# The split tables of the TensorE picks in another layout: the part index outermost

## The chip, the core and the metric

The kernel runs on one core of a Trainium2 chip. Its engines are TensorE (PE, with its weight load shown apart as PEld), VectorE (DVE), ScalarE (ACT), GpSimd (POOL) and SyncE (SP); each has its own queue of instructions, and they meet through semaphores. The metric is the device time of one execution in microseconds, as the median of several runs.

## The reference, cut to what matters

A graph of 12500 nodes (64 features) and 400000 edges, sorted by destination. Two layers follow each other, each with a residual and a layer norm:

```python
h    = x @ W_lin + b_lin
agg1 = mean over edges into a node of h[src]
h    = tanh(agg1 @ W1_agg + h @ W1_root + b1)            # 16 wide
agg2 = mean over edges into a node of h[src]
x    = layernorm(x + tanh(agg2 @ W2_agg + h @ W2_root + b2))
hn   = x @ Wn.T + bn
w    = ssp(ssp(edge_attr @ We1.T + be1) @ We2.T + be2)   # per edge, 64 wide
agg  = segment_sum(hn[src] * w, dst)
x    = layernorm(x + (ssp(agg @ Wc.T + bc) @ Wp.T + bp))
```

So rows of a node table are fetched by `src` three times (tables p1, h1 and hn) and added up by `dst`.

## The kernel before

The edges are cut into 125 blocks (`NB`) of 128 partitions x 25 slots. Three phases go over all blocks: `pick_phase("e1")` on the p1 table, `pick_phase("e2")` on the h1 table (both 16 numbers a row), `gate_phase("e3")` on the hn table (64 numbers). Phase A before e1 builds the p1 table, phase B between e1 and e2 the h1 table, phase C between e2 and e3 the first layer norm and the hn table, phase D the output.

The row of an edge's source is fetched in one of two ways. For the first 15 slots of a block in the pick phases (23 in the gate phase) GpSimd issues one indirect DMA a slot from DRAM (L612, L886). For the last 10 slots (`SEL`; `GSEL` = 2 in the gate phase) TensorE picks the row from a copy of the table in SBUF, by one-hot matmuls. The 98 rows that a partition holds (`NQ`) stand in `split_sb` (`hn_split` in the gate phase), padded to 100 in the pick phases. Each number is split into two parts (upper 12 bits of the fraction, and the rest), so that a matmul of type fp32r is exact. A row index q is taken as two digits: in the pick phases h = q mod 4 and a = q div 4 (25 values). For each h and each part one matmul streams the 25 rows of that h (400 columns) against the one-hot weight `low_hot[:, h]` and adds into one PSUM bank (L667, 8 matmuls a slot); a ninth (L670) streams `others`, 400 numbers in one run, against `hi_hot` and pushes the 24 rows that are not a down by a large number; VectorE then takes the maximum over a (`take`, L719). In the gate phase h = q mod 7, a = q div 7 (14 values, in two halves of 7 rows, 448 columns, into two banks, L921, 28 matmuls a slot), and VectorE masks and sums over a. In `split_sb` of before, the two parts of a row lie side by side and rows are in order, so what a matmul reads is 25 runs of 16 numbers, 128 numbers apart; in `hn_split` 7 runs of 64.

The digits are made once by VectorE in phase A (L446 to L476), turned by TensorE and stored as f16 rows (`sel_dram`, `gate_dram`). Per block SyncE loads them broadcast over partitions, ScalarE makes `low_hot` (four `Abs` activations on L633, one `Relu` on L637), VectorE makes `hi_hot` (L712).

The fetched and picked rows are added up by destination: VectorE writes one-hot tiles `hot` of 13 and 12 slots for a window of 128 destinations (L739, `make_hot`), TensorE multiplies the rows with them (`add_up`, L685, 25 matmuls of 128 columns), VectorE adds the sum into `acc` (L765). A block whose destinations span two windows has two visits, with 50 matmuls; how many a block has is read at run time. The later a block, the wider its destinations are spread.

The order of TensorE's work is written out by hand. In the body of block n: `pick(0, n+1)`, then `add_up(n)`, then `pick(1)`, `pick(2)`, `pick(3)` of n+1, the four groups having 3, 2, 3 and 2 slots (`SIZE`). VectorE's body: first one-hot tile of n, `take(3, n)`, `high_hots`, the split of the picked rows into bf16 parts (L725 to L731), the visits, then `take(0)` to `take(2)` of n+1. GpSimd's gathers go up to four blocks ahead in the pick phases (two in the gate phase) and wait for `block_used`; `add_up(n)` waits for the gathers of block n.

`table_rows` (L246) writes both the bf16 rows for DRAM and `split_sb`; the gate phase's `hn_split` is written on L1376 (VectorE) and L1412 (ScalarE).

Of the kernel before, what the change touches and what calls it, by code (L numbers as in the profile page):

```python
# [24 lines left out]
F = 64  # L25
# [59 lines left out]
def gnn_kernel(nc, x, xw, src, src_sel, dst_all, edge_t, W_linT, b_lin, W1_agg, W1_root, b1, W2_parts, W2_diag, WnT, bn, We1T, be1,  # L85
               We2T, be2, WcT, bc, WpT, bp, out):
    ctx = ExitStack()
    with ctx:
# [108 lines left out]
        split_sb = mid.enter_context(nc.sbuf_tensor("split_sb", [P, HI1 * HI2, 2 * H], F32R))  # L197
# [48 lines left out]
        def table_rows(dve, v, rows, split, top_i, low_n, made):  # L246
# [9 lines left out]
            dve.tensor_copy(split[..., 0:H], top_i.bitcast(F32))  # L256
            dve.drain()
            dve.tensor_copy(part(MID), low_n)
            dve.tensor_tensor(split[..., H:2 * H], v, top_i.bitcast(F32), ALU.subtract)
# [29 lines left out]
        with nc.Block() as block:  # L289
# [135 lines left out]
            def _(dve):  # L425
# [7 lines left out]
                for w in range(2):  # L433
# [8 lines left out]
                dve.tensor_scalar(split_sb[:, NQ:, :].rearrange("p a c -> p (a c)"), others_f[:, 0:4, :]  # L442
                                  .rearrange("p a f -> p (a f)"), 0.0, None, ALU.mult)
# [15 lines left out]
                dve.tensor_single_scalar(gate_i[:, :, :], sel_a_i[:, SEL - GSEL:, :], 147, ALU.mult)  # L459
                dve.drain()  # L460
                dve.tensor_single_scalar(gate_i[:, :, :], gate_i[:, :, :], 10, ALU.arith_shift_right)
                dve.drain()
                dve.tensor_copy(gate_hi[:, :, :].rearrange("p n j -> p j n"), gate_i[:, :, :])
                dve.drain()
                dve.scalar_tensor_tensor(gate_low[:, :, :], gate_hi[:, :, :].rearrange("p n j -> p j n"), -float(GLOW),
                                         sel_q[:, SEL - GSEL:, :], ALU.mult, ALU.add)
                dve.drain()
                dve.scalar_tensor_tensor(gate_low[:, :, :], gate_low[:, :, :], float(P), sel_digit[0][:, SEL - GSEL:, :],
                                         ALU.mult, ALU.add)
                dve.tensor_single_scalar(sel_a_i[:, :, :], sel_a_i[:, :, :], HI2.bit_length() - 1, ALU.arith_shift_right)  # L470
# [3 lines left out]
                dve.scalar_tensor_tensor(sel_q[:, :, :], sel_digit[1], -float(HI2), sel_q[:, :, :], ALU.mult, ALU.add)  # L474
                dve.drain()
                dve.scalar_tensor_tensor(sel_digit[0], sel_q[:, :, :], float(P), sel_digit[0], ALU.mult, ALU.add)  # L476
# [4 lines left out]
                for c in range(2):  # L481
                    if c == 1:
# [8 lines left out]
                               halves(split_sb[:, 0:NQ, :])[:, :, a:b, :],  # L491
# [51 lines left out]
        def pick_phase(tag, table, buf, hots, tiles):  # L543
# [33 lines left out]
            with nc.Block() as block:  # L577
# [75 lines left out]
                def _(pe):  # L653
# [4 lines left out]
                    def pick(gr, n):  # L658
# [3 lines left out]
                        for k in range(SIZE[gr]):  # L662
                            e = slice(k * P, (k + 1) * P)
                            o = bank[BANK0[gr] + k][:, 0:PICK]
                            for h in range(HI2):
                                for part in range(2):
                                    pe.matmul(o, low_hot[gr][:, h, e],  # L667
                                              split_sb[:, h:HI1 * HI2:HI2, part * H:(part + 1) * H],
                                              start=(h == 0 and part == 0), stop=False)
# [120 lines left out]
        def gate_phase(tag, table, buf, hots, tiles):  # L790
# [52 lines left out]
            with nc.Block() as block:  # L843
# [49 lines left out]
                def _(pe):  # L893
# [21 lines left out]
                    def pick(n, s):  # L915
                        pe.wait_ge(low_made, GSEL * n + s + 1)
                        pe.wait_ge(pick_taken, GSEL * n + s + 1)
                        for h in range(GLOW):
                            for part in range(2):
                                for c in range(2):  # L920
                                    last = pe.matmul(bank[c][:, 0:GHALF * F], low_hot[s][:, h, :],  # L921
                                                     hn_split[:, c * GHALF * GLOW + h:(c + 1) * GHALF * GLOW:GLOW,
# [727 lines left out]
```

## Time and profile before

| | us |
|---|---|
| median of 3 runs | 9292.74 |
| lowest and highest | 9292.62, 9294.54 |
| span of the profiled execution | 9281.8 |
| median less span | 10.9 |

| engine | busy us | share of the span | instructions |
|---|---|---|---|
| PE | 8512.6 | 92% | 52035 |
| PEld | 7831.7 | 84% | 52036 |
| DVE | 6294.8 | 68% | 7500 |
| ACT | 5654.9 | 61% | 10182 |
| POOL | 6536.9 | 70% | 6717 |

The span runs from the first to the last instruction of one profiled execution; its own time as a run is not given apart. The busy time of PE is modelled at its ends: matmuls are pipelined, so the mean of one (358 ns for L667) is longer than the distance between the starts of two; where a distance is meant, it is read from starts. The phases lie at about 71 to 2665 us (e1), 2737 to 5330 us (e2) and 5470 to 9210 us (e3). The granted TensorE clock is a share of 2.4 GHz; its mean over the span is 0.952.

### The profile page before, as it was taken

Reading aid. Unit: us, or ns where it says so; the run is one execution under the profiler, and the core shown is the slowest. Engines: PE = TensorE matmul, PEld = TensorE weight load, DVE = VectorE, ACT = ScalarE, POOL = GpSimd, SP = SyncE. Lnnn points to the kernel's source line nnn. Section 1 sums busy time; section 2 is a strip of 40 time slices with the busy share of each in tenths; the row PEclk is TensorE's granted clock in tenths of the full one; section 3 lists DMA queues with packets and bytes.
Section 4 is the critical chain, followed back from the end, with each engine's and each line's share of the span. In section 5 each row is a group of like instructions: output and inputs, shape, how many; then the busy total and the mean of one; then the engine's idle time right before and its main releaser. Section 6 shows DMA issues by size and latency. Waiting matters only on the chain. (4 is left out here: it accounts for less than half of the span.)

```text
span 9281.8 us, 165856 instructions
## 1 busy us (share of the span) xinstructions
PE 8512.6 (92%) x52035; PEld 7831.7 (84%) x52036; DVE 6294.8 (68%) x7500; ACT 5654.9 (61%) x10182; POOL 6536.9 (70%) x6717
## 2 busy tenths in 40 slices
PE   8999999988889999999898878888888888999998
PEld 7999999888889999998888867677777777888887
DVE  6666666767756666667767766666666666777777
ACT  5666666555546666665555456666666666666665
POOL 5777777756637777777666447777777777777776
PEclk9999999999989999999999979999999999999998
DMA  2222222111112222222111122222222222222222
GB/s 74 50 48 48 49 49 48 40 38 39 39 30 51 48 48 50 48 48 45 41 36 39 28 76 54 57 57 57 53 57 57 57 57 54 57 57 57 53 57 57
DMA packets 385189, 466.16 MB, mean 50 GB/s; under 512 B 174821, under 2 KB 253241, under 8 KB 384742
## 3 DMA queue, kind: packets, MB, share of 16 engines
q0 software_dynamic: 212000, 156.07, 10.9%
q1 hardware_dynamic: 172804, 309.29, 10.2%
q8 instruction: 32, 0.52, 0.0%
q14 instruction: 31, 0.25, 0.0%
q10 hardware_dynamic: 322, 0.03, 0.0%
HBM read 451.33 MB, written 13.55 MB: 50 GB/s over the span
## 5 line engine op out<-in xcount | busy, mean ns | idle before, releaser
L667 PE MATMUL banks<-split_sb,e_low_hot 128*128 128x400 f32 x20000 | 4283.7, 358 | 28.8 <-ACT e_low_hot L637 28.8
L667 PEld LDWEIGHTS banks<-split_sb,e_low_hot 128*128 128x128 f32 x20000 | 3799.5, 192 | 70.5 <-ACT e_low_hot L637 29.2
L886 POOL DMA_INDIRECT big<-hn_table,src_i x2875 | 2852.3, 992 | 884.8 <-issue 869.3
L637 ACT ACTIVATE e_low_hot<-e_key_off 128x1536 fp32r<-128x1536 f16 x1000 | 1272.2, 1272 | 1854.6 <-PE banks L670 1823.5
L612 POOL DMA_INDIRECT big<-p_table,src_i x1875 | 1806.7, 964 | 785.1 <-issue 559.0
L612 POOL DMA_INDIRECT big<-h_table,src_i x1875 | 1806.3, 963 | 727.3 <-issue 554.7
L719 DVE TENSOR_REDUCE picked<-banks 128x48 f32<-128x1200 f32 x1000 | 1194.2, 1194 | 1205.1 <-PE banks L670 1202.3
L633 ACT ACTIVATE e_key_off<-e_key_in,node_off 128x384 f16<-128x384 f16 (+1 forms) x4000 | 1920.9, 551 | 103.5 <-DMA e_hi_in<-sel_dram 21.9
L739 DVE SCALAR_TENSOR_TENSOR hot<-dst_f,win_base,banks 128x1536 bf16<-128x1536 f32 (+1 forms) x934 | 1762.3, 1896 | 308.8 <-issue 180.1
L921 PE MATMUL banks<-hn_split,e_low_hot 128*128 128x448 f32 x7000 | 1488.1, 369 | 73.5 <-issue 68.0
L921 PEld LDWEIGHTS banks<-hn_split,e_low_hot 128*128 128x128 f32 x7000 | 1299.5, 188 | 202.0 <-issue 63.8
L938 PEld LDWEIGHTS banks<-hot,big 128*64 128x64 f32 x8550 | 929.7, 137 | 155.0 <-issue 122.8
L938 PE MATMUL banks<-hot,big 128*64 128x128 f32 x8550 | 982.8, 274 | 49.6 <-DVE acc L1117 30.0
L1080 DVE SCALAR_TENSOR_TENSOR hot<-dst_f,win_base,banks 128x1664 f32<-128x1664 f32 (+1 forms) x467 | 885.2, 1896 | 178.0 <-PE banks L938 126.2
L670 PE MATMUL banks<-others,e_hi_hot 128*128 128x400 f32 x2500 | 866.2, 346 | 0.0
L685 PE MATMUL banks<-hot,big 128*64 128x128 bf16 x8550 | 600.7, 226 | 245.4 <-DVE acc L765 153.3
L904 PE MATMUL banks<-e_wide,we 128*128 128x512 f32 x1000 | 546.5, 709 | 298.4 <-DVE e_wide L1046 288.4
L685 PEld LDWEIGHTS banks<-hot,big 128*64 128x64 bf16 x8550 | 516.3, 114 | 355.7 <-DVE hot L739 271.5
L970 ACT ACTIVATE e_wide<-e_wide 128x512 f32<-128x512 f32 x500 | 268.9, 538 | 859.3 <-DVE e_wide L1046 859.3
L999 ACT ACTIVATE e_low_hot<-e_key_in,node_off 128x128 fp32r<-128x128 f16 x1750 | 537.0, 387 | 348.4 <-PE banks L921 346.9
L904 PEld LDWEIGHTS banks<-e_wide,we 128*128 128x128 f32 x1000 | 253.7, 262 | 538.0 <-DVE e_wide L1046 353.4
L1092 DVE SCALAR_TENSOR_TENSOR big<-e_wide,big 128x1600 f32<-128x1600 f32 x125 | 228.3, 1826 | 643.2 <-DMA big<-hn_table,src_i 639.2
(212 smaller groups left out, 5936.4 us busy)
## 6 DMA issues: line engine op xcount, KB each, us to landing
e_wide<-in_edge_t SPq DMA_DIRECT2D x125, 832.0 KB
e_key_in<-sel_dram SPq DMA_DIRECT2D x250, 320.0 KB
e_hi_in<-sel_dram SPq DMA_DIRECT2D x250, 320.0 KB
big<-hn_table,src_i POOLq DMA_INDIRECT x2875
big<-p_table,src_i POOLq DMA_INDIRECT x1875
big<-h_table,src_i POOLq DMA_INDIRECT x1875
e_key_in<-gate_dram SPq DMA_DIRECT2D x125, 64.0 KB
src_i<-in_src SPq DMA_DIRECT2D x375, 12.5 KB, 1.7
```

What stands on the lines that cost most here:

```text
L612: pool.indirect_dma_start(buf[u][:, j, 0:ROW0], None, table, bass.IndirectOffsetOnAxis(ap=src_i[u][:, j:j + 1], axis=0),).then_inc(gathere ...
L633: act.activation(off[:, h, :], key_in[u][:, es], ACT.Abs, bias=node_off[:, h:h + 1])
L637: act.activation(low_hot[gr][:, :, :], off, ACT.Relu, bias=1.0, scale=-1.0).then_inc(low_made, 1)
L667: pe.matmul(o, low_hot[gr][:, h, e], split_sb[:, h:HI1 * HI2:HI2, part * H:(part + 1) * H], start=(h == 0 and part == 0), stop=False)
L670: last = pe.matmul(o, hi_hot[gr][:, e], others[:, :, :], start=False, stop=True)
L685: last = pe.matmul(sums[0:ROW0, 0:WIN], buf[u][:, j, :], hots[h][:, j - a, :], start=(j == 0), stop=(j == SLOTS - 1))
L719: dve.tensor_reduce(picked[:, AT[gr]:AT[gr] + SIZE[gr], :], found, AX.X, ALU.max).then_inc(pick_taken, 1)
L739: dve.scalar_tensor_tensor(hots[h], d.unsqueeze(2).to_broadcast([P, b - a, WIN]), win_base[:, bass.ds(window, 1)], iota_ps.unsqueeze(1).to ...
L886: pool.indirect_dma_start(buf[u][:, j, 0:F], None, table, bass.IndirectOffsetOnAxis(ap=src_i[u][:, j:j + 1], axis=0),).then_inc(gathered[u ...
L921: last = pe.matmul(bank[c][:, 0:GHALF * F], low_hot[s][:, h, :], hn_split[:, c * GHALF * GLOW + h:(c + 1) * GHALF * GLOW:GLOW, part * F:(p ...
L938: last = pe.matmul(sums[0:F, 0:WIN], buf[u][:, j, 0:F], hots[h][:, j - a, :], start=(j == 0), stop=(j == SLOTS - 1))
L1080: dve.scalar_tensor_tensor(hots[h], d.unsqueeze(2).to_broadcast([P, b - a, WIN]), win_base[:, bass.ds(window, 1)], iota_ps.unsqueeze(1).to ...
```

## The change

Both split tables get the part index outermost and the rows of one h next to each other: `split_sb[:, part, row, :]` and `hn_split[:, part, row, :]`. For the rows of one h to be neighbours while the table itself stays in order, the digits change places: h = q div 25 and a = q mod 25 in the pick phases, h = q div 14 and a = q mod 14 in the gate phase. So the digits are computed by other constants (41/1024 is 1/25, 2341/32768 is 1/14 for these q). A matmul then reads rows h * 25 to h * 25 + 24 of one part. The number of matmuls, their columns and their order stay the same. The diff is whole.

```diff
@@ -194,7 +194,7 @@
         root = mid.enter_context(nc.sbuf_tensor("root", [P, NQ, H], F32))
         h1_deg = mid.enter_context(nc.sbuf_tensor("h1_deg", [P, NQ, H + 1], F32))
         deg = mid.enter_context(nc.sbuf_tensor("deg", [P, NQ], F32))
-        split_sb = mid.enter_context(nc.sbuf_tensor("split_sb", [P, HI1 * HI2, 2 * H], F32R))
+        split_sb = mid.enter_context(nc.sbuf_tensor("split_sb", [P, 2, HI1 * HI2, H], F32R))
 
         banks = pb("banks", [P, 8 * 512])
         bank = [banks[:, i * 512:(i + 1) * 512] for i in range(8)]
@@ -253,10 +253,10 @@
             dve.tensor_single_scalar(top_i, v.bitcast(I32), TOP12, ALU.bitwise_and)
             dve.drain()
             dve.tensor_tensor(low_n, v, part(HI), ALU.subtract)
-            dve.tensor_copy(split[..., 0:H], top_i.bitcast(F32))
+            dve.tensor_copy(split[0], top_i.bitcast(F32))
             dve.drain()
             dve.tensor_copy(part(MID), low_n)
-            dve.tensor_tensor(split[..., H:2 * H], v, top_i.bitcast(F32), ALU.subtract)
+            dve.tensor_tensor(split[1], v, top_i.bitcast(F32), ALU.subtract)
             dve.drain()
             dve.tensor_tensor(part(LO), low_n, part(MID), ALU.subtract).then_inc(made, 1)
 
@@ -439,8 +439,8 @@
                 dve.tensor_copy(bias_wide[:, :, :], bias_1[:, :].unsqueeze(1).to_broadcast([1, 16, 2 * H])).then_inc(a_w, 1)
                 dve.wait_ge(consts, 1)
                 dve.tensor_copy(others[:, :, :], others_f)
-                dve.tensor_scalar(split_sb[:, NQ:, :].rearrange("p a c -> p (a c)"), others_f[:, 0:4, :]
-                                  .rearrange("p a f -> p (a f)"), 0.0, None, ALU.mult)
+                dve.tensor_scalar(split_sb[:, :, NQ:, :], others_f[:, 0:2 * (HI1 * HI2 - NQ), :]
+                                  .rearrange("p (s a) f -> p s a f", s=2), 0.0, None, ALU.mult)
                 dve.wait_ge(sel_src_in, 16)
                 src_n = sel_src_i.rearrange("p (j n) -> p j n", n=NB)
                 dve.tensor_single_scalar(sel_p_i, sel_src_i, 1, ALU.arith_shift_right)
@@ -456,24 +456,26 @@
                 dve.drain()
                 dve.tensor_copy(sel_a_i[:, :, :], sel_q[:, :, :])
                 dve.drain()
-                dve.tensor_single_scalar(gate_i[:, :, :], sel_a_i[:, SEL - GSEL:, :], 147, ALU.mult)
-                dve.drain()
-                dve.tensor_single_scalar(gate_i[:, :, :], gate_i[:, :, :], 10, ALU.arith_shift_right)
-                dve.drain()
-                dve.tensor_copy(gate_hi[:, :, :].rearrange("p n j -> p j n"), gate_i[:, :, :])
-                dve.drain()
-                dve.scalar_tensor_tensor(gate_low[:, :, :], gate_hi[:, :, :].rearrange("p n j -> p j n"), -float(GLOW),
+                dve.tensor_single_scalar(gate_i[:, :, :], sel_a_i[:, SEL - GSEL:, :], 2341, ALU.mult)
+                dve.drain()
+                dve.tensor_single_scalar(gate_i[:, :, :], gate_i[:, :, :], 15, ALU.arith_shift_right)
+                dve.drain()
+                dve.tensor_copy(gate_low[:, :, :], gate_i[:, :, :])
+                dve.drain()
+                dve.scalar_tensor_tensor(gate_hi[:, :, :].rearrange("p n j -> p j n"), gate_low[:, :, :], -float(GHIGH),
                                          sel_q[:, SEL - GSEL:, :], ALU.mult, ALU.add)
-                dve.drain()
                 dve.scalar_tensor_tensor(gate_low[:, :, :], gate_low[:, :, :], float(P), sel_digit[0][:, SEL - GSEL:, :],
                                          ALU.mult, ALU.add)
-                dve.tensor_single_scalar(sel_a_i[:, :, :], sel_a_i[:, :, :], HI2.bit_length() - 1, ALU.arith_shift_right)
+                dve.tensor_single_scalar(sel_a_i[:, :, :], sel_a_i[:, :, :], 41, ALU.mult)
+                dve.drain()
+                dve.tensor_single_scalar(sel_a_i[:, :, :], sel_a_i[:, :, :], 10, ALU.arith_shift_right)
                 dve.drain()
                 dve.tensor_copy(sel_digit[1], sel_a_i[:, :, :])
                 dve.drain()
-                dve.scalar_tensor_tensor(sel_q[:, :, :], sel_digit[1], -float(HI2), sel_q[:, :, :], ALU.mult, ALU.add)
-                dve.drain()
-                dve.scalar_tensor_tensor(sel_digit[0], sel_q[:, :, :], float(P), sel_digit[0], ALU.mult, ALU.add)
+                dve.scalar_tensor_tensor(sel_q[:, :, :], sel_digit[1], -float(HI1), sel_q[:, :, :], ALU.mult, ALU.add)
+                dve.scalar_tensor_tensor(sel_digit[0], sel_digit[1], float(P), sel_digit[0], ALU.mult, ALU.add)
+                dve.drain()
+                dve.tensor_copy(sel_digit[1], sel_q[:, :, :])
                 dve.drain()
                 dve.sem_inc(sel_digits, 1)
 
@@ -488,7 +490,7 @@
                     a, b = ACUT[c], ACUT[c + 1]
                     dve.wait_ge(a_p1, c + 1)
                     table_rows(dve, halves(p1_n[:, :, :])[:, :, a:b, :], halves(tab[:, :, :])[:, :, a:b, :],
-                               halves(split_sb[:, 0:NQ, :])[:, :, a:b, :],
+                               [halves(split_sb[:, part, 0:NQ, :])[:, :, a:b, :] for part in range(2)],
                                top[:, 0:2 * (b - a), :].rearrange("p (w i) h -> p w i h", w=2),
                                low[:, 0:2 * (b - a), :].rearrange("p (w i) h -> p w i h", w=2), a_tab)
 
@@ -664,8 +666,7 @@
                             o = bank[BANK0[gr] + k][:, 0:PICK]
                             for h in range(HI2):
                                 for part in range(2):
-                                    pe.matmul(o, low_hot[gr][:, h, e],
-                                              split_sb[:, h:HI1 * HI2:HI2, part * H:(part + 1) * H],
+                                    pe.matmul(o, low_hot[gr][:, h, e], split_sb[:, part, h * HI1:(h + 1) * HI1, :],
                                               start=(h == 0 and part == 0), stop=False)
                             last = pe.matmul(o, hi_hot[gr][:, e], others[:, :, :], start=False, stop=True)
                         last.then_inc(pick_psum, 1)
@@ -919,8 +920,7 @@
                             for part in range(2):
                                 for c in range(2):
                                     last = pe.matmul(bank[c][:, 0:GHALF * F], low_hot[s][:, h, :],
-                                                     hn_split[:, c * GHALF * GLOW + h:(c + 1) * GHALF * GLOW:GLOW,
-                                                              part * F:(part + 1) * F],
+                                                     hn_split[:, part, h * GHIGH + c * GHALF:h * GHIGH + (c + 1) * GHALF, :],
                                                      start=(h == 0 and part == 0), stop=(h == GLOW - 1 and part == 1))
                         last.then_inc(pick_psum, 1)
 
@@ -1198,7 +1198,7 @@
                     if c > 0:
                         dve.wait_ge(b_h, c)
                         a, b = BCUT[c - 1], BCUT[c]
-                        table_rows(dve, root[:, a:b, :], tab[:, a:b, :], split_sb[:, a:b, :], top[:, 0:b - a, :],
+                        table_rows(dve, root[:, a:b, :], tab[:, a:b, :], [split_sb[:, part, a:b, :] for part in range(2)], top[:, 0:b - a, :],
                                    low[:, 0:b - a, :], b_tab)
 
             @block.scalar
@@ -1254,7 +1254,7 @@
         f_out = sem("f_out")
         f_store = [sem(f"f_store{b}") for b in range(2)]
         hn_held = ExitStack()
-        hn_split = hn_held.enter_context(nc.sbuf_tensor("hn_split", [P, NQ, 2 * F], F32R))
+        hn_split = hn_held.enter_context(nc.sbuf_tensor("hn_split", [P, 2, NQ, F], F32R))
         f_top = sem("f_top")
         f_hi = sem("f_hi")
         f_xb = sem("f_xb")
@@ -1373,7 +1373,7 @@
                     dve.tensor_single_scalar(t, hn_o[g % 2][:, 0:b - a, :].bitcast(I32), TOP12,
                                              ALU.bitwise_and).then_inc(f_top, 1)
                     dve.drain()
-                    dve.tensor_tensor(hn_split[:, a:b, F:2 * F], hn_o[g % 2][:, 0:b - a, :], t.bitcast(F32), ALU.subtract)
+                    dve.tensor_tensor(hn_split[:, 1, a:b, :], hn_o[g % 2][:, 0:b - a, :], t.bitcast(F32), ALU.subtract)
 
                 for g in range(NGQ + 2):
                     if g < NGQ:
@@ -1409,7 +1409,7 @@
                     if g >= 3:
                         a, b = group(g - 3)
                         act.wait_ge(f_top, g - 2)
-                        act.copy(hn_split[:, a:b, 0:F], top_i[(g - 3) % 2][:, 0:b - a, :].bitcast(F32)).then_inc(f_hi, 1)
+                        act.copy(hn_split[:, 0, a:b, :], top_i[(g - 3) % 2][:, 0:b - a, :].bitcast(F32)).then_inc(f_hi, 1)
 
             @block.gpsimd
             def _(pool):
```

## Rows read from the trace of the kernel before

**Rows 1.** The page, part 1: busy us (share of the span) xinstructions.

```profile
PE 8512.6 (92%) x52035; PEld 7831.7 (84%) x52036; DVE 6294.8 (68%) x7500; ACT 5654.9 (61%) x10182; POOL 6536.9 (70%) x6717
```

**Rows 2.** The page, part 5: costliest groups, count, busy us, mean ns, idle before.

```profile
L667 PE MATMUL banks<-split_sb,e_low_hot 128*128 128x400 f32 x20000 | 4283.7, 358 | 28.8 <-ACT e_low_hot L637 28.8
...
L886 POOL DMA_INDIRECT big<-hn_table,src_i x2875 | 2852.3, 992 | 884.8 <-issue 869.3
...
L612 POOL DMA_INDIRECT big<-p_table,src_i x1875 | 1806.7, 964 | 785.1 <-issue 559.0
...
L921 PE MATMUL banks<-hn_split,e_low_hot 128*128 128x448 f32 x7000 | 1488.1, 369 | 73.5 <-issue 68.0
...
L685 PE MATMUL banks<-hot,big 128*64 128x128 bf16 x8550 | 600.7, 226 | 245.4 <-DVE acc L765 153.3
```

**Rows 3.** Timeline, phase e1, one-visit blocks: start us, duration us, engine, line.

```profile
102.29 0.91 PE L685 MATMUL banks<-hot,big 128*64 128x128 bf16 x13
...
88.85 0.96 POOL L612 DMA_INDIRECT big<-p_table,src_i  x1 [0.30 <-issue]
...
1461.24 1.63 PE L685 MATMUL banks<-hot,big 128*64 128x128 bf16 x25
...
1458.41 0.98 POOL L612 DMA_INDIRECT big<-p_table,src_i  x1 [0.30 <-issue]
```

**Rows 4.** Timeline of PE, phase e1, first matmul of five add-ups of two visits.

```profile
2072.59 0.30 PE L685 MATMUL banks<-hot,big 128*64 128x128 bf16 x2
...
2095.53 0.24 PE L685 MATMUL banks<-hot,big 128*64 128x128 bf16 x1
...
2261.97 0.24 PE L685 MATMUL banks<-hot,big 128*64 128x128 bf16 x1
...
2287.65 0.24 PE L685 MATMUL banks<-hot,big 128*64 128x128 bf16 x1
...
2574.43 0.35 PE L685 MATMUL banks<-hot,big 128*64 128x128 bf16 x3
```

**Rows 5.** Timeline of DVE in the same stretch.

```profile
2238.60 1.95 DVE L739 SCALAR_TENSOR_TENSOR hot<-dst_f,win_base,banks 128x1664 bf16<-128x1664 f32 x1 [0.54 <-PE banks L685]
```

**Rows 6.** Timeline of PE: one add-up of two visits, and the pick after it.

```profile
2237.53 1.58 PE L685 MATMUL banks<-hot,big 128*64 128x128 bf16 x25
...
2243.93 1.04 PE L667 MATMUL banks<-split_sb,e_low_hot 128*128 128x400 f32 x2
```

**Rows 7.** Windows: length, busy us (xcount) by engine, PEclk, DMA share, GB/s.

```profile
2218.65:2222.06 3.41, 3.41 (x15) 3.22 (x13) 3.08 (x4) 0.00 (x0) 1.43 (x2) 0.50 0.01 3
...
2266.45:2273.25 6.80, 6.30 (x27) 6.10 (x28) 4.25 (x5) 0.00 (x0) 2.86 (x3) 0.50 0.04 5
...
2338.15:2341.50 3.35, 2.94 (x17) 2.76 (x18) 3.25 (x4) 0.00 (x0) 0.22 (x1) 0.50 0.00 0
```

**Rows 8.** Windows by stage: phase e1 in two parts, and phase e3.

```profile
75.00:1580.00 1505.00, 1491.22 (x9126) 1452.30 (x9126) 1032.64 (x1270) 1027.03 (x1609) 1143.16 (x1188) 1.00 0.21 49
...
1580.00:2665.00 1085.00, 976.55 (x6350) 939.05 (x6350) 760.05 (x859) 569.29 (x891) 660.50 (x685) 0.95 0.16 37
...
5470.00:9210.00 3740.00, 3322.06 (x19710) 2844.50 (x19711) 2494.75 (x2884) 2346.47 (x5001) 2852.30 (x2875) 0.94 0.24 56
```

**Rows 9.** Timeline of PE: one pick of nine matmuls in phase e1.

```profile
2256.79 1.69 PE L667 MATMUL banks<-split_sb,e_low_hot 128*128 128x400 f32 x8
2258.31 0.35 PE L670 MATMUL banks<-others,e_hi_hot 128*128 128x400 f32 x1
2258.49 1.68 PE L667 MATMUL banks<-split_sb,e_low_hot 128*128 128x400 f32 x8
```

**Rows 10.** Timeline of PE: one pick of phase e3.

```profile
6005.49 5.92 PE L921 MATMUL banks<-hn_split,e_low_hot 128*128 128x448 f32 x28
```

**Rows 11.** Timeline of DVE in phase A.

```profile
21.07 0.81 DVE L472 CAST hot<-sel_a_i 128x1250 f32<-128x1250 int32 x1
...
29.16 0.56 DVE L252 CAST a_tab<-p_n 128x768 bf16<-128x768 f32 x1 [4.20 <-ACT p_n L368]
```

## The prediction

> **What bounds the kernel now.** I read the page's groups first, then the windows by stage, then single blocks in the timeline of TensorE, GpSimd and VectorE. By share of the span TensorE is the bound: busy 92% [rows 1], and half the span is the 20000 pick matmuls of L667, with 7000 more on L921 [rows 2]. The share is an average over stages with different limits, so I ask in each stage what ends last.
>
> Stage one, pick phases, blocks of one visit (two thirds of each phase). GpSimd issues 15 gathers a block. In a pick phase they are 1806.7 us busy and 559.0 us idle in "issue", the fixed pause between two of them [rows 2], so 2365.7 / 1875 = 1.262 us each and 18.9 us a block; counted over whole blocks the beat is 19.02. TensorE needs a little less: at the start its add-up begins 102.29 - 88.85 = 13.4 us behind the last gather's issue of its block, 72 blocks later 1461.24 - 1458.41 = 2.8 us behind [rows 3]. So its block is (1461.24 - 102.29) / 72 = 18.87 us, it catches up 0.15 us a block, and at 2.8 us it meets the gather's landing and from there keeps GpSimd's pace. It is already at that floor before the two-visit blocks begin.
>
> Stage two, the blocks of two visits. 8550 matmuls on L685 are 342 visits of 25 [rows 2]; 250 blocks in two phases, so 92 blocks have two. Here a block takes (2574.43 - 2072.59) / 21 = 23.90 us [rows 4], more than GpSimd's 19, so GpSimd runs four buffers ahead and waits. A block without a drop of the clock takes 2095.53 - 2072.59 = 22.94 us [rows 4]. In it TensorE is the bound: all ten picks stand in its chain, and VectorE's hot tile for the second visit waits 0.54 us for TensorE's first add-up [rows 5]. During the add-ups TensorE works little: two bursts of 25 short matmuls from 2237.53 to about 2243.9, waiting for VectorE between them [rows 6]. There the granted clock falls to its low level of 1.2 GHz for 3.4 or 6.8 us [rows 7], and what falls on picks runs at half pace: the block that starts at 2237.53 lasts 24.44 us, to 2261.97 [rows 4], so one drop costs 1.5 us. The stage's clock is 0.95, stage one's 1.00 [rows 8].
>
> Stage three, the gate phase: 2875 gathers, 2852.3 us busy plus 869.3 in "issue" of 884.8 idle [rows 2] = 3721.6 us of a stage of 3740 [rows 8]. GpSimd never waits for anybody here worth naming. TensorE's picks on L921 are hidden.
>
> **What the change removes.** The spacing of the picks, start to start. Eight strided matmuls of L667 go from 2256.79 to 2258.31, 0.190 each; the one of L670, which reads 400 numbers in one run from `others`, is followed after 2258.49 - 2258.31 = 0.18 us [rows 9]. On L921, 28 matmuls of 448 columns in 7 runs: (5.92 - 0.37) / 27 = 0.206, the first of them longer, so about 0.204 for the others [rows 10]; scaled by columns to 400 that is 0.182. So one run or seven cost about the same per column, and 25 runs some 7 ns more. I take 0.183 us for the changed L667, by the nearest row, L670: 6.5 ns x 8 = 52 ns a pick, 0.52 us a block. Bounds: 0 from above (the spacing has another cause, below). From below the pace of L685, 128 columns in (1.58 - 0.22) / 24 = 0.057 us [rows 6], times 400/128 = 0.177: 13 ns each, 1.04 us a block. A loss I cannot exclude from a row, but every operand in one run that the trace has is the faster one.
> L921: from 7 runs to one I take 0; the bound is the same 0.177 per 400 columns, 5 ns a matmul, and hidden behind GpSimd at any size.
>
> **Where that lies.** In stage one it lies beside GpSimd's gathers. TensorE catches up 0.15 + 0.52 = 0.67 us a block instead of 0.15, meets the landing after some 16 blocks instead of 72, and then waits. The two-visit blocks start at the same time as now: 0. What is late next is the gather. If that cover were gone, 158 blocks x 0.52 = 82 us would count.
> In stage three: 0, same cover.
> In stage two it is on the chain, all ten picks: VectorE's slack of 0.54 us [rows 5] must take the 0.26 us of the five picks between VectorE's take and the first add-up, and does. That is 92 x 0.52 = 48 us at an unchanged clock, and here is the step that I weigh most. The low stretches begin at 2218.65, 2266.45 and 2338.15 [rows 7]: 47.80 = 2 x 23.90 and 71.70 = 3 x 23.90 us apart, and 23.90 is also the mean block. Blocks of 22.94, 24.44 and (with a drop of 6.8 us) 2287.65 - 2261.97 = 25.68 us [rows 4] alternate so that their mean stays on this beat: a block without a drop comes early to the next one, whose add-up then lies where it earns a drop, and is set back. That is a regulator: what picks save brings more drops. With the change a block without a drop is 22.94 - 0.52 = 22.42, one with a single drop 22.42 + 1.5 = 23.92: still the beat, now with a drop in nearly every block instead of in some 60%. So I forecast that the clock takes the 48 us back but for about 3. It holds only by a hair: 1 ns of spacing is 80 ns a block, and 23.92 stands against 23.90.
>
> **The small edits.** The key digits: VectorE does one 1250-wide shift and one 1250-wide copy more (the multiply takes the place of a shift, and a copy is added), 2 x 0.81 = 1.6 us [rows 11], before L252, where VectorE waits 4.20 us for ScalarE [rows 11]: 0, cover left 2.6 us; uncovered it would be 1.6 us once. The splits are written with as many elements by as many instructions (L256, L259, L1376, L1412), and 768 wide they take what any such copy takes, so 0, and in any case between -1 and +1 us for all of them. The zeroing of the spare rows is one instruction as before. The host's side and all DMAs are unchanged. GpSimd's pace is a touch quicker where TensorE waits for it; some 50 more blocks in that state, at 0.03 to 0.06 us each, are 2 to 3 us.
>
> Sum: 3 + 3 = 6 us. The span of the profiled execution is 9281.8 us; the median of the runs lies 10.9 us above it, for what lies around the span, so 9275.8 + 10.9 = 9286.7 us. Its own range: 9276 to 9293.
>
> **A rule against the change.** L670 against L667 shows a difference of some 7 ns [rows 9]. The Trainium skill, "SBUF — State Buffer", Specifications (TRN2), says that SBUF is read in lines of 16 bytes and that full speed needs two or more hits in a line, each change of line costing something. A run of 16 numbers of 4 bytes is four full lines, so old and new layout touch the same 100 lines with four hits each. By that rule the spacing stays at 190 ns and the time at about 9292.
>
> **The rivals.**
> 1. No change of spacing, chance 0.17. L670 and L921 differ from L667 in more than their runs: the matmul after each of them writes another PSUM bank, while the eight of L667 accumulate into one. If that is the 6.5 ns, the layout does nothing. For it: position is confounded with run length in every row I have. Against: L685 accumulates into one bank at 0.057 per 128 columns [rows 6] and shows no such extra. Time 9292, 9289 to 9296. The line rule above would give this too.
> 2. The beat lets go, chance 0.31. If the new spacing is below about 182.5 ns, a block with one drop is shorter than 23.90, and the add-ups drift through the beat; many blocks get no drop at all. With none, a block is 22.42: (23.90 - 22.42) x 92 = 136 us; with drops in as many blocks as now, 48 us. Middle 80 us: 9213, from 9160 to 9265. For it: 22.42 + 1.5 is only just the beat, and L921 scaled gave 0.182. Against: L670's row at 0.18 to 0.19 within its rounding.
> 3. Slower, chance 0.08. The pick before the add-up ends earlier while VectorE's chain stays, so TensorE's thin stretch of 6.4 us grows by 0.26. If this makes the low stretch 6.8 us instead of 3.4 in a third of the two-visit blocks, each pays 25.68 - 24.44 = 1.24 us more: 31 x 1.24 = 38 us: 9324. From 15 blocks on it is slower by over 0.2%. For it: such double drops are there now [rows 7]. Against: a double drop sets the block far back, and the next one has none.
> 4. The forecast, chance 0.44.
>
> **How the numbers follow.** A measurement here can tell about 0.2%, 18.6 us, from no change. Faster: rival 2 nearly whole and the edge of the forecast, 0.33. Slower: rival 3 and a little for what I don't see, 0.09. Same: 0.58. Time 9286. Range 9190 to 9300: it leaves out the far half of rival 2 and rival 3. Forecast and rival 1 alone: 9276 to 9296.
>
> **What would show it.** Eight matmuls of L667 in 1.47 us instead of 1.52 (right), still 1.52 (rival 1), under 1.46 (rival 2's door). TensorE behind GpSimd's last issue by 2.8 us from about block 16. The two-visit block: mean 23.90 with granted clock under 0.95 (the regulator), mean near 22.5 to 23.3 and a higher clock (rival 2), above 24 (rival 3). The gate stage within a few us. I am wrong if the stage from 75 to 1580 us ends earlier by more than 5 us, for then GpSimd was not its floor.

## The result, and the profile after

The changed kernel takes 9205.86 us, median of 4 runs (9197.64 to 9214.44), against 9293.64 (9292.62 to 9294.78, 4 runs): ratio 0.9905 [0.9893, 0.9917], 88 us less. The forecast was 9286, so next to nothing gained, and that was wrong in kind. The time lies inside the range of 9190 to 9300 only because the range reached over rival 2, "the beat lets go" (9213, chance 0.31), and that is what happened. The profiled execution after took 9197.64 us.

The page of after, parts 1 and 5, against [rows 1, 2]:

```profile
PE 8324.8 (91%) x52035; PEld 7644.7 (83%) x52036; DVE 6283.8 (68%) x7502; ACT 5655.1 (62%) x10182; POOL 6542.3 (71%) x6717
...
L669 PE MATMUL banks<-split_sb,e_low_hot 128*128 128x400 f32 x20000 | 4091.5, 347 | 30.5 <-ACT e_low_hot L639 30.5
L887 POOL DMA_INDIRECT big<-hn_table,src_i x2875 | 2854.2, 993 | 884.1 <-issue 869.6
L922 PE MATMUL banks<-hn_split,e_low_hot 128*128 128x448 f32 x7000 | 1489.5, 369 | 73.3 <-issue 68.0
```

What moved is one row: L667, now L669, is busy for 192 us less. The kernel gains 88. The windows of after by stage (length, busy us by engine, PEclk, DMA share, GB/s) answer to [rows 8]:

```profile
75.00:1580.00 1505.00, 1436.74 (x9138) 1401.58 (x9138) 1027.09 (x1270) 1027.11 (x1609) 1142.69 (x1189) 1.00 0.21 49
1580.00:2617.00 1037.00, 933.40 (x6340) 894.52 (x6338) 759.68 (x858) 569.36 (x891) 661.71 (x684) 0.97 0.16 39
...
5383.00:9123.00 3740.00, 3325.13 (x19707) 2843.12 (x19708) 2494.07 (x2884) 2346.41 (x5001) 2854.18 (x2875) 0.94 0.23 56
```

Stage one: TensorE has 54 us less work in the same 1505 us, and it goes into waiting. Stage two: the same work is done in 1037 us instead of 1085, at a clock of 0.97 instead of 0.95. Stage three: 3740 us for the same gathers. Counted by starts, the first two-visit block of phase e1 begins 0.8 us earlier, and the last pick of the phase 47.6 us earlier. Here is that pick, in the timeline of TensorE before and after:

```profile
2663.66 0.34 PE L670 MATMUL banks<-others,e_hi_hot 128*128 128x400 f32 x1
```

```profile
2616.02 0.34 PE L671 MATMUL banks<-others,e_hi_hot 128*128 128x400 f32 x1
```

In phase e2 the one-visit blocks take 2.6 us more than before, and the last pick comes 87.0 us earlier. The gate phase takes 3729.6 us from its first to its last gather, before 3728.6. All of the gain is in the two-visit blocks.

A pick of after, timeline of TensorE, against [rows 9]; it starts again after 1.63 us, before after 1.70:

```profile
2101.90 1.61 PE L669 MATMUL banks<-split_sb,e_low_hot 128*128 128x400 f32 x8
2103.34 0.34 PE L671 MATMUL banks<-others,e_hi_hot 128*128 128x400 f32 x1
2103.53 1.61 PE L669 MATMUL banks<-split_sb,e_low_hot 128*128 128x400 f32 x8
```

Over all picks at full clock the spacing of two L669 is 180.6 ns (17027 of them), before 189.6. In the two-visit stage, the first matmuls of five add-ups in a row, against [rows 4]:

```profile
2116.63 0.91 PE L686 MATMUL banks<-hot,big 128*64 128x128 bf16 x13
...
2138.88 0.91 PE L686 MATMUL banks<-hot,big 128*64 128x128 bf16 x13
...
2161.12 0.91 PE L686 MATMUL banks<-hot,big 128*64 128x128 bf16 x13
...
2183.47 1.89 PE L686 MATMUL banks<-hot,big 128*64 128x128 bf16 x25
...
2207.26 1.75 PE L686 MATMUL banks<-hot,big 128*64 128x128 bf16 x25
```

Blocks of 22.25, 22.24, 22.35 and 23.79 us: three in a row with hardly a price for the clock, then one that pays 1.5 for a drop (a stretch in which the granted clock is at its low level). Before, the blocks swung around 23.90. Low stretches are still there, with the same level as in [rows 7] (windows of after):

```profile
2188.96:2192.37 3.41, 3.41 (x16) 3.21 (x14) 3.14 (x4) 0.00 (x0) 1.41 (x2) 0.51 0.02 2
2257.26:2260.67 3.41, 3.41 (x16) 3.22 (x14) 3.22 (x4) 0.00 (x0) 1.14 (x2) 0.51 0.00 0
2281.16:2284.57 3.41, 3.41 (x15) 3.22 (x13) 3.11 (x4) 0.00 (x0) 1.42 (x2) 0.51 0.01 2
```

The last two lie 23.90 us apart, as before; the first two 68.3, with free blocks between. Before there were 24 and 23 low stretches in the two pick phases, now there are 15 and 19.

### The profile page after: what moved, and what is told of

It is laid out like the page before. It is cut to its first block and busy times, and to the rows that moved or that the text cites. A ratio compares the mean times of both kernels' runs of the same rounds, so it can differ in the third digit from the quotient of the medians.

```text
span 9195.2 us, 165858 instructions
## 1 busy us (share of the span) xinstructions
PE 8324.8 (91%) x52035; PEld 7644.7 (83%) x52036; DVE 6283.8 (68%) x7502; ACT 5655.1 (62%) x10182; POOL 6542.3 (71%) x6717
## 5 line engine op out<-in xcount | busy, mean ns | idle before, releaser
L669 PE MATMUL banks<-split_sb,e_low_hot 128*128 128x400 f32 x20000 | 4091.5, 347 | 30.5 <-ACT e_low_hot L639 30.5
L669 PEld LDWEIGHTS banks<-split_sb,e_low_hot 128*128 128x128 f32 x20000 | 3668.5, 190 | 57.0 <-ACT e_low_hot L639 30.9
```

Source lines behind the costliest of these rows:

```text
L669: pe.matmul(o, low_hot[gr][:, h, e], split_sb[:, part, h * HI1:(h + 1) * HI1, :], start=(h == 0 and part == 0), stop=False)
```

## The experiments

Times are medians; the kernel before ran on the same chip each time. Theory A: the 25 runs cost the time by themselves. Theory B: something that came with them does (the order of the table, the distance of the runs, the new digits). Theory C, on top of either: the clock takes savings back up to some size.

**1. Only the outer order of the table, runs as before.** The kernel before, with part outermost:

```diff
-split_sb [P, HI1 * HI2, 2 * H]      read [:, h:HI1 * HI2:HI2, part * H:(part + 1) * H]
+split_sb [P, 2, HI1 * HI2, H]       read [:, part, h:HI1 * HI2:HI2, :]
```

> The kernel before with the part index outermost in the pick phases only and the old digits: a pick matmul reads 25 runs of 16 numbers, now 64 apart and not 128. Theory (the number of runs sets the spacing): still 0.189 to 0.190 us between picks, time 9285 to 9300. Rival (the part beside it, or the 128 apart, was the trouble): 0.181, time near 9206.

Measured: 9284.17 (9279.07 to 9285.58, 8 runs) against 9283.98: 0.9999 [0.9989, 1.0009]. Spacing 189.4 ns. The outer order does nothing, and neither does halving the distance between two runs from 128 numbers to 64. (The times of this experiment and the next lie a few us under what I expected, because I had set that from the first chip; on this one the kernel before takes 9284 and not 9293.)

**2. The new digits, but 25 runs, 32 numbers apart.** The changed kernel with the table as it was:

```diff
-split_sb[:, part, h * HI1:(h + 1) * HI1, :]
+split_sb[:, h * HI1:(h + 1) * HI1, part * H:(part + 1) * H]
```

> The changed kernel with the parts of split_sb side by side again, the new digits kept: 25 runs of 16 numbers, 32 apart. Theory (number of runs): 0.189 to 0.190 us between picks, 9285 to 9300. Rival (the exchange of the digits, so other one-hot weights, brought the gain): 0.181 and 9206. Rival (lines that the matmul skips cost, neighbouring ones do not): between 0.181 and 0.189.

Measured: 9281.97 (9279.35 to 9284.25, 8 runs): 0.9998 [0.9988, 1.0008]. Timeline of TensorE in this kernel and in experiment 1, one pick each:

```profile
2197.38 1.67 PE L669 MATMUL banks<-split_sb,e_low_hot 128*128 128x400 f32 x8
2198.88 0.34 PE L671 MATMUL banks<-others,e_hi_hot 128*128 128x400 f32 x1
2199.06 1.67 PE L669 MATMUL banks<-split_sb,e_low_hot 128*128 128x400 f32 x8
```

```profile
2151.54 1.68 PE L667 MATMUL banks<-split_sb,e_low_hot 128*128 128x400 f32 x8
2153.07 0.34 PE L670 MATMUL banks<-others,e_hi_hot 128*128 128x400 f32 x1
2153.24 1.68 PE L667 MATMUL banks<-split_sb,e_low_hot 128*128 128x400 f32 x8
```

1.68 and 1.70 us, against 1.63: one run alone is what matters (A). The mean spacing is 188.2 ns, so runs that lie nearer are 1.2 ns cheaper. That should be 0.13 us a block, 12 us in 92; the median moved 2, which the interval does not tell from nothing. Add-ups of two visits in this kernel, first matmuls:

```profile
2117.08 1.58 PE L686 MATMUL banks<-hot,big 128*64 128x128 bf16 x25
...
2141.38 1.58 PE L686 MATMUL banks<-hot,big 128*64 128x128 bf16 x25
...
2167.00 1.58 PE L686 MATMUL banks<-hot,big 128*64 128x128 bf16 x25
...
2189.82 0.91 PE L686 MATMUL banks<-hot,big 128*64 128x128 bf16 x13
...
2212.65 1.58 PE L686 MATMUL banks<-hot,big 128*64 128x128 bf16 x25
```

24.30, 25.62, 22.82, 22.83, and then the same four again: mean 23.89, as before 23.91. The regulator that I predicted is here, and it holds fully (C): the blocks show it, where the median alone could not.

**3. Half of the picks in one run.** In part 1 the rows of h and its partner alternate, part 0 is as changed:

```diff
-split_sb[:, part, h * HI1:(h + 1) * HI1, :]
+part 0: the same;  part 1: split_sb[:, 1, at:at + 2 * HI1, :].rearrange("p (a k) c -> p k a c", k=2)[:, h % 2]
```

> The changed kernel, but part 1 of split_sb is stored with two values of h interleaved row by row, so that four of the eight matmuls of a pick read 25 runs and four read one. Both theories give 0.185 us for the mean spacing. If the time follows the spacing (half of the change): 9293 - 44 = 9249. If the beat of 23.90 us holds the two-visit blocks until a block with one drop is shorter than the beat (22.94 - 0.36 + 1.45 = 24.03 is still longer): two-visit blocks of 23.85 to 23.90 with a drop in nearly each, time 9287 to 9294, no gain.

Measured: 9255.1 (9253.4 to 9259.7, 7 runs): 0.9968 [0.9957, 0.998]. The eight matmuls of a pick take 1.483 us, exactly the mean of experiment 2 (1.511) and of after (1.455): the cost is per strided matmul. Add-ups, first matmuls:

```profile
2111.39 1.70 PE L707 MATMUL banks<-hot,big 128*64 128x128 bf16 x25
...
2133.93 1.59 PE L707 MATMUL banks<-hot,big 128*64 128x128 bf16 x25
...
2158.01 1.59 PE L707 MATMUL banks<-hot,big 128*64 128x128 bf16 x25
...
2182.08 0.91 PE L707 MATMUL banks<-hot,big 128*64 128x128 bf16 x13
...
2206.09 1.90 PE L707 MATMUL banks<-hot,big 128*64 128x128 bf16 x25
...
2230.05 1.87 PE L707 MATMUL banks<-hot,big 128*64 128x128 bf16 x25
...
2253.97 0.91 PE L707 MATMUL banks<-hot,big 128*64 128x128 bf16 x13
```

22.54, then 24.08, 24.07, 24.01, 23.96, 23.92: each block pays a drop and glides onto 23.9 until one slips through, and three blocks of 22.55 follow. Of 86 two-visit blocks in the two phases 28 are free of a drop. The hold lets most of the saving through here, with a one-drop block of 24.0, where I had set full hold and no gain for anything over 23.90; the time is near the 9249 that I had set for the spacing alone. What the runs give for what the picks save: 12 us at constant clock gave 2, 37 (0.40 x 92) gave 29, and the whole change's 66 gave 74 (experiment 5) and 88.

**4. The gate table back to 7 runs of 64.** The changed kernel, with hn_split as before:

```diff
-hn_split[:, part, h * GHIGH + c * GHALF:h * GHIGH + (c + 1) * GHALF, :]
+hn_split[:, h * GHIGH + c * GHALF:h * GHIGH + (c + 1) * GHALF, part * F:(part + 1) * F]
```

> The changed kernel with only hn_split laid out as before (7 runs of 64 for the matmuls of the gate phase). Theory (GpSimd's gathers are the floor of the gate phase, and 7 runs cost no more than one): gate phase within 3 us of the changed kernel's, time 9198 to 9214. Rival (part of the gain is in the gate phase): more than 9220.

Measured: 9225.97 (9174.39 to 9227.67, 5 runs): 0.9938 [0.9922, 0.9955]. Its gate phase takes 29.80 us a block, after 29.85, and the spacing there is 203.65 ns, after 203.77: seven runs or one are the same. The median lies outside the 9198 to 9214 that I expected and above the 9220 that I had set for a gain in the gate phase. By the trace of its fastest run the 20 us to after's median are not the gate's. This kernel's pick phases are after's to the instruction, and its five runs spread over 53 us (9174, 9206, 9226, 9226, 9228). No trace of one of the slower runs was kept, so that their time too is lost in the pick phases is inferred. How often the add-ups slip past a drop differs from one execution to the next: the profiled one, the fastest at 9174, has 9 and 17 low stretches in its pick phases, against 15 and 19 in after's.

**5. The changed kernel again**, unchanged, on another chip, beside the next three.

> The changed kernel once more, on the chip of the three beside it. The drops are not held to a beat, so single executions should lie 10 to 40 us apart: median 9195 to 9225. Theory (the gate phase is no part of the gain): the same as the kernel with only the gate table laid out as before.

Measured: 9209.64 (9192.74 to 9220.23, 4 runs) against 9283.58: 0.9923 [0.9906, 0.9939]. Reproduced, spread 27 us; the kernel before spreads 8 in 13 runs there.

**6 and 7. Fill TensorE's thin stretches.** Four matmuls of 400 columns, whose result nobody reads, stand between the two bursts of each add-up, in the changed kernel and in the kernel before:

```diff
+if h == 1:
+    for _ in range(4):
+        pe.matmul(bank[5][:, 0:PICK], hi_hot[0][:, 0:P], others[:, :, :], start=True, stop=True)
```

> The changed kernel with four more matmuls of 400 columns between the two bursts of each add-up, into a PSUM bank that nobody reads, so that TensorE is not thinly loaded there; the result is the same. Theory (the drops of the clock in the two-visit blocks cost what lies above a block of 22.24 us): hardly a drop left in the pick phases, two-visit blocks of 22.2 to 22.4 instead of 22.9, one-visit blocks unchanged at 19.0 under GpSimd's gathers: 9130 to 9160. Rival (what lies above 22.24 us is not the clock): two-visit blocks longer by the fill, 9210 to 9280.

> The kernel before with the same four matmuls in each visit. Theory: two-visit blocks of 22.9 to 23.1 us with hardly a drop (23.88 without the fill), so that the spacing alone is worth 0.7 us a block between this and the changed kernel with the fill; but one-visit blocks go from 19.0 to about 19.6, as TensorE has only 0.15 us a block to spare there, so the time is 9200 to 9290.

Measured: 9197.64 (9196.28 to 9199.15, 4 runs), 0.991 [0.9893, 0.9926], and 9379.69 (9378.14 to 9381.24, 2 runs), 1.0105 [1.0085, 1.0125]. The windows of the two-visit stage, first of the filled changed kernel, then of the filled one before:

```profile
1600.00:2600.00 1000.00, 961.61 (x6529) 904.93 (x6527) 747.04 (x840) 566.53 (x887) 647.64 (x671) 1.00 0.17 40
```

```profile
1660.00:2700.00 1040.00, 1000.94 (x6596) 939.10 (x6596) 751.86 (x849) 565.72 (x886) 623.68 (x639) 1.00 0.16 38
```

The clock is 1.00 in both: it is the thin work around the add-ups that lets it fall. And with no drop, every block is alike. Add-ups, first matmuls, 15 blocks apart, in the same order:

```profile
1991.01 0.91 PE L690 MATMUL banks<-hot,big 128*64 128x128 bf16 x13
...
2330.49 0.69 PE L690 MATMUL banks<-hot,big 128*64 128x128 bf16 x9
```

```profile
2061.22 0.91 PE L689 MATMUL banks<-hot,big 128*64 128x128 bf16 x13
...
2411.45 0.74 PE L689 MATMUL banks<-hot,big 128*64 128x128 bf16 x10
```

339.48 / 15 = 22.63 and 350.23 / 15 = 23.35 us: the layout by itself is worth 0.72 us a block. Both forecasts of the time missed. For the filled changed kernel I had expected 9130 to 9160, from blocks of 22.2 to 22.4 us; the drops are gone, but the block is 22.63 and not the drop-free 22.24 of after, so the fill itself costs 0.4 us a block and takes back more than half of what the drops had cost. For the filled kernel before I had expected 9200 to 9290: the fill also stands in the one-visit blocks, where TensorE has next to no slack, and makes them 19.76 us, so that the two-visit stage starts 69 us later (add-up of block 78 at 1644.5 us, before at 1575.0). Twice 69, less 92 x (23.90 - 23.35) = 51, is 88 of the 96 us that it lost. With the new layout the same fill gives 19.04, just over GpSimd's pace. The filled changed kernel has the lowest median of all, 12 us under the changed one beside it, which the two intervals don't tell from nothing; it is steadier, with a spread of 3 us against 27.

**8. Two of 15 gathers left out (kernel before).** GpSimd's cover of stage one is taken away; the rows are set to zero.

```diff
-took = SLOTS - SEL
+took = SLOTS - SEL - 2
+dve.memset(buf[u][:, took:SLOTS - SEL, :], 0.0)
```

> The kernel before, leaving out two of the fifteen gathers of each block of the pick phases (their rows are left at zero). GpSimd then needs 16.5 us a block. Theory (one-visit blocks are under GpSimd, TensorE close below): one-visit blocks of 18.85 us in both pick phases, time some 2 x 3 us less, 9275 to 9290 and two-visit blocks at 23.9 as before.

Measured: 9269.3 (9263.26 to 9272.87, 8 runs): 0.9984 [0.9974, 0.9995], some 14 us less, more than I had set. In its timeline GpSimd now waits, for the sequencer of VectorE:

```profile
989.38 0.95 POOL L612 DMA_INDIRECT big<-p_table,src_i  x1 [2.60 <-DVEq L766]
990.64 0.95 POOL L612 DMA_INDIRECT big<-p_table,src_i  x1 [0.31 <-issue]
```

The one-visit block is 18.79 us, TensorE's own, where it was 18.87 beside the gathers; two-visit blocks stay at 23.91. So stage one before has two limits within 0.25 us: 18.79 for TensorE and 19.02 for GpSimd. A cheaper pick alone can move nothing there.

**9 to 12. Fill only in the gap between two visits, and 13 gathers with the new layout.** Seven fill matmuls after the first visit's add-up, none in one-visit blocks, in after, before and half; and experiment 8's edit on the changed kernel.

```diff
+with pe.If(visit + 1 < to):
+    for _ in range(7):
+        pe.matmul(bank[5][:, 0:PICK], hi_hot[0][:, 0:P], others[:, :, :], start=True, stop=True)
```

> The changed kernel with seven more matmuls of 400 columns into an unread bank after every visit but a block's last, so only in the 1.8 us in which TensorE waits for VectorE between two visits; the result is the same. Theory (what lies above a two-visit block of 22.24 us is the clock): no drop, blocks of 22.25 to 22.4, one-visit blocks at 18.97 to 19.03 under GpSimd, time 9284 - 90 x 1.55 = 9145 (9130 to 9160). Rival (the fill puts off the second visit): 22.6 and more, 9180 and more.

> The kernel before with the same fill between two visits. Theory: 22.95 to 23.05 in each two-visit block and no drop, time 9284 - 90 x 0.9 = 9203 (9195 to 9215), as fast as the layout alone. Rival (the beat is not made by the clock): 23.9 and 9280.

> The kernel with one of the two parts in one run, and the fill between two visits. Theory: with the clock held the gain follows the spacing, pick by pick: 22.55 to 22.65 a two-visit block, time 9166 to 9178, so some 60% of the way from the filled kernel before to the filled changed one. Rival (the step between half and whole is more than the spacing): nearer to the filled kernel before, above 9190.

> The changed kernel, leaving out two of the fifteen gathers of each block of the pick phases (their rows are left at zero). Theory (the change's gain in the one-visit blocks is hidden under GpSimd): one-visit blocks of 18.1 us instead of 19.0, against 18.79 of the kernel before with 13 gathers; time 9060 to 9090, 180 to 200 below that kernel. Rival (something else holds them at 19): above 9180.

Measured on another chip, where every kernel, the one before too (13358.17 us, 29 runs), takes 44% longer, with a mean granted clock of 0.81 to 0.83 against 0.95: 13348.31 (0.9995 [0.998, 1.001]), 13356.3 (0.9995 [0.9983, 1.0007]), 13351.52 (0.9996 [0.9987, 1.0006]) and 12709.33 (0.9514 [0.9492, 0.9537]). These runs don't answer what they were made for, and none of the four times can be held against what I expected of it. There TensorE stops in the middle of picks with nothing that it waits for (timeline, gap fill on the changed kernel):

```profile
1013.07 2.83 PE L669 MATMUL banks<-split_sb,e_low_hot 128*128 128x400 f32 x8 [2.63 <-issue]
...
1019.31 0.34 PE L669 MATMUL banks<-split_sb,e_low_hot 128*128 128x400 f32 x1 [1.17 <-issue]
1020.71 1.45 PE L669 MATMUL banks<-split_sb,e_low_hot 128*128 128x400 f32 x7 [1.06 <-issue]
```

In its groups that is 1065.2 us of idle "issue" before L669, where after has 30.5 us idle in all. No gain of the shorter spacing is left in the times there:

```profile
L669 PE MATMUL banks<-split_sb,e_low_hot 128*128 128x400 f32 x20000 | 4622.9, 370 | 1257.7 <-issue 1065.2
```

Two blocks a phase tell something all the same: the last gather of e1 is issued at 3790.32 us, and from then on blocks run as on the other chips, here with the fill in the gap:

```profile
3820.36 1.58 PE L686 MATMUL banks<-hot,big 128*64 128x128 bf16 x25
3821.87 1.54 PE L691 MATMUL banks<-others,e_hi_hot 128*128 128x400 f32 x7
3823.70 0.91 PE L686 MATMUL banks<-hot,big 128*64 128x128 bf16 x13 [0.29 <-DVE acc L770]
...
3842.61 0.58 PE L686 MATMUL banks<-hot,big 128*64 128x128 bf16 x7
```

3842.61 - 3820.36 = 22.25 us, a block without a drop of after (22.24): seven fill matmuls between the visits cost nothing. The same block takes 22.99 us in the gap-filled kernel before and 22.55 in the gap-filled half, much as drop-free blocks do without a fill (22.95 and 22.55). Whether they keep the clock up on an ordinary chip, and bring back the 61 us (92 x 0.66) that drops still cost there, stays open.

## Where the prediction was right, and where wrong

**Where the time lies: right.** Stage one and the gate gave nothing, as the cover by the gathers said: 0.8 us earlier in e1, 2.6 us later in e2, and the gate 1.0 us longer. TensorE meets the gathers at block 17, predicted 16. Add-up and last issue of that block, timeline of TensorE and of GpSimd:

```profile
415.86 0.52 PE L686 MATMUL banks<-hot,big 128*64 128x128 bf16 x6
```

```profile
412.90 0.96 POOL L614 DMA_INDIRECT big<-p_table,src_i  x1 [0.31 <-issue]
```

The lag is 3.0 us there and 2.9 at block 72 (1460.36 against 1457.47), as in [rows 3]. That 16 was so near is luck: with the 0.72 us a block that the picks save (below) it would have been block 12. By the starts of the add-ups in the trace of after, blocks 1 to 12 take 18.40 us each, before 18.85, so a one-visit block saves only 0.45; TensorE now waits 0.22 us a block inside the add-up, before 0.06, and where a wait is named it is for VectorE's one-hot tile. The small edits came out as next to nothing. The 3 us that the sum had for a quicker pace of GpSimd did not come.

**The size of the spacing: the first failure.** The step took "0.183 us for the changed L667, by the nearest row, L670" [rows 9]; the measured mean is 180.6 ns, 9.0 under before instead of 6.5. The reading of the row was good: over all its picks at full clock L670 is followed after 183.1 ns before. What failed is the step from L670 to L667. L670's follower is a matmul that opens another bank, and it still stands at 182 ns after, where the eight of L669 stand at 180.6; the nearest row was not the same thing. In a block the change is worth 0.72 us (experiments 6 and 7), not 0.52: 92 x 0.72 = 66 us, not 48.

**The regulator: the second failure, and the one that decides.** The forecast was that "the clock takes the 48 us back but for about 3"; instead the clock took nothing back and gave some on top. "23.92 stands against 23.90" was a hold by a hair. With 180.6 ns a block with one drop is 22.24 + 1.5 = 23.8, under the 23.90, and rival 2's condition (spacing under 182.5) was met: mean two-visit blocks of 22.88 and 22.93 in the two phases, from 23.91 and 23.85. For the 86 blocks counted that is 83 of the 88 us: 61 from the picks at constant clock (0.71 each) and 22 from fewer drops (0.92 us a block before, 0.67 after). That there is such a regulator was right: experiment 2 loses its 12 us to it, and experiment 3 a part of its own. What was off is the edge, and not by a hair: the hold does not end at 23.90, since in experiment 3, with a one-drop block of 24.0 above it, a third of the blocks slip through and 29 of 37 us come out. The spacing of 183 that I had set lies between that experiment and the change, so by these two neighbours the forecast would have failed at its own spacing as well; no run has that spacing. Rival 2 named the condition and nearly the size, but its upper bound of 9265 lies above its own 9293 - 48 = 9245.

**Rival 1 is out** (L670 and its bank as the cause): experiments 1 and 2 keep the banks and the order of the matmuls, and only the runs make 188 to 189 into 181 ns. With it falls what I drew from the Trainium skill, "SBUF — State Buffer", Specifications (TRN2), lines of 16 bytes read at full speed with two hits in each: all layouts here touch 100 full lines for 400 numbers, and they differ by 7.6 to 9.0 ns. Runs of 64 numbers show no such cost (203.65 against 203.77 ns), so the price is that of many short runs; at 25 runs that is 0.3 to 0.4 ns a run. **Rival 3 is out:** drops of 6.8 us became fewer, from 12 in the two pick phases to 4.

**Left open:** why a run of 16 costs TensorE's reading something and a run of 64 nothing; why the hold of the clock lets go between one-drop blocks of 24.3 us (experiment 2) and 24.0 (experiment 3); and the odd chip. How long a one-visit block would be if the gathers did not cover it at all is not shown either, as the run for it (experiment 12) fell on that chip. That fp32r picks of the two parts are exact is the intent of the kernel; no run here measures it.

## What to carry to other kernels

Where a matmul's moving operand is picked out of a table, lay the table out so that it is one long run; short runs cost some per cent of the pick, and long enough ones nothing. Work out a saving stage by stage from what ends last there, then ask what the clock does with it: in a loop whose idle stretches let the clock fall, small savings can vanish and larger ones come back with interest. A copy of the loop that is filled so that the clock stays up shows what an edit is worth without the clock, but the fill has a price of its own. Rank such edits by medians of several runs, since single executions of the changed kernel lay up to 27 us apart, and those of experiment 4, with the same pick phases, 53.

## What the runs showed of the hardware that I had not expected

- Four matmuls with unread results in each add-up hold the granted clock at 1.00 in the two-visit stage, every block alike; without them it is 0.95 [rows 8] in the kernel before and 0.97 in the changed one.
- At the low clock the layout does not matter: picks stand 333 ns apart there in all kernels with 400 columns, against 181 or 190 at full clock: the cost of the runs is gone when TensorE itself goes at half pace.
- One chip ran all of this 44% slower, with stalls of 1 to 3 us inside picks that end when the gathers end; leaving out 2 of 15 gathers won 4.9% there (changed kernel) and 0.2% elsewhere (kernel before). The two go together; that the gathers cause the stalls was not shown.
